# Attention arithmetic on pairs of token tiles, with the projection, the transposes and the index conversions re-ordered around it

## The reference

```
mod = silu(c) @ wmod -> sa, ca, ga, sb, cb, gb        (ga, gb kept at least 0.25 away from zero)
h = layernorm(x) * (1 + ca) + sa
a = groupnorm( tanh( relu( rope(h @ W_Q) ) + hh_b ) )  (32 groups of 16 channels; rope on the first 64 channels)
x = x + ga * transpose(a)                              (tokens and channels swapped, read back as B,T,C)
h = layernorm(x) * (1 + cb) + sb
x = x + gb * ( (silu(h @ Wg.T) * (h @ Wu.T)) @ Wd.T )  (Wg, Wu, Wd: 1376 x 512, each entry lut[idx], 16 table values)
```

## Time and profile before

| | |
|---|---|
| median of 3 runs | 1054.35 us (1053.17 to 1059.23) |
| profiled execution | 1054.04 us, its span 1051.8 us |
| PE busy | 943.4 us, 90% of the span |
| DVE busy | 602.9 us, 57% |
| ACT busy | 414.1 us, 39% |
| POOL busy | 185.0 us, 18% |

### The profile page before, as it was taken

One profiled execution on the slowest core, in us unless ns is written; L12 is line 12 of the kernel. 1 busy time (PEld: TensorE's weight loads), 2 busy tenths in 40 slices (PEclk: granted clock), 3 DMA queues, 4 the chain that ended last, 5 costly groups with the idle time before them and its releaser, 6 DMA issues.

```text
span 1051.8 us, 12874 instructions
## 1 busy us (share of the span) xinstructions
PE 943.4 (90%) x4364; PEld 435.4 (41%) x4364; DVE 602.9 (57%) x1375; ACT 414.1 (39%) x627; POOL 185.0 (18%) x156
## 2 busy tenths in 40 slices
PE   5777569877898979999898899999999999999998
PEld 1233334333343434444444444444444444444443
DVE  5896999975888953335878876322222432222312
ACT  3482857483665633224552532222222421222200
POOL 3130202053565632012211200110000100000000
PEclk8889698998999999999999999999999999999999
DMA  8659356410000031124235214222000112000011
GB/s 272 180 139 309 75 177 202 117 55 26 21 30 20 20 120 61 44 97 121 58 102 160 40 41 160 81 79 82 0 0 1 61 41 100 0 0 0 1 41 41
DMA packets 33738, 83.44 MB, mean 79 GB/s; under 512 B 2848, under 2 KB 2976, under 8 KB 30624
## 3 DMA queue, kind: packets, MB, share of 16 engines
q1 hardware_dynamic: 32544, 74.54, 21.4%
q0 software_dynamic: 1152, 8.39, 4.3%
HBM read 64.04 MB, written 18.87 MB: 79 GB/s over the span
## 4 chain that ended last, share of the span: by engine, by line
PE 65%; DVE 18%; issue 6%; ACT 6%; POOL 2%; DMA 2%; SPq 1%; DVEq 0%; ACTq 0%; POOLq 0%
PE ps L1191 28%; PE ps L1225 22%; PE ps L1158 6%; DVE hid L854 3%; PE ps L1180 3%; DVE R L876 2%; PE ps L1203 2%; PE ps L1146 2%; DVE st L770 1%; DMA xa<-x_dram 1%; DVE hd L885 1%; ACT R L578 1%; ACT h L517 1%; DVE xa L865 1%; POOL work L434 1%
## 5 line engine op out<-in xcount | busy, mean ns | idle before, releaser
L1191 PE MATMUL ps<-h,w_all 128*128 128x512 f16 x1920 | 424.8, 383 | 18.8 <-DVE hd L885 16.3
L1191 PEld LDWEIGHTS ps<-h,w_all 128*128 (+1 forms) x1920 | 188.6, 99 | 252.3 <-issue 19.9
L1225 PE MATMUL ps<-w_all,hid 128*128 128x512 f16 x1056 | 231.1, 381 | 4.7 <-DVE w_all L1075 4.7
L1225 PEld LDWEIGHTS ps<-w_all,hid 128*128 128x128 f16 x1056 | 103.5, 98 | 129.6 <-DVE w_all L1075 5.2
L885 DVE SCALAR_TENSOR_TENSOR hd<-ps,col,sg 128x512 f32<-128x512 f32 x80 | 59.8, 748 | 154.7 <-ACT sg L539 154.7
L539 ACT ACTIVATE sg<-ps,col 128x512 f32<-128x512 f32 x80 | 54.6, 682 | 181.8 <-PE ps L1191 181.2
L910 DVE SCALAR_TENSOR_TENSOR hd<-ps,col,gbB 128x512 f32<-128x512 f32 x32 | 24.0, 751 | 148.4 <-PE ps L1225 148.1
L1180 PE MATMUL ps<-hid,w_all 128*128 128x512 f16 x352 | 90.8, 422 | 12.1 <-DVE hid L854 11.1
L554 ACT ACTIVATE hid<-hd 128x512 f16<-128x512 f32 (+1 forms) x88 | 55.0, 628 | 112.9 <-DVE hd L885 99.6
L1158 PE MATMUL ps<-WQ,work 128*128 128x512 f16 x384 | 89.7, 396 | 7.0 <-POOL work L434 7.0
L434 POOL TENSOR_TENSOR h<-h,h 128x512 f16<-128x512 f32 x32 | 37.4, 1188 | 306.2 <-ACT h L524 306.2
(11 more groups left out here) (115 smaller groups left out, 786.3 us busy)
## 6 DMA issues: line engine op xcount, KB each, us to landing
R<-x_dram SPq DMA_DIRECT2D x16, 1024.0 KB, 6.9
xa<-x_dram SPq DMA_DIRECT2D x14, 1024.0 KB, 6.1
hid<-idx_dram SPq DMA_DIRECT2D x44, 256.0 KB, 5.6
R<-bias_dram POOLq DMA_DIRECT2D x8, 1024.0 KB, 8.3
out_dram<-R SPq DMA_DIRECT2D x32, 256.0 KB, 2.2
x_dram<-R SPq DMA_DIRECT2D x7, 1024.0 KB, 5.1
w_all<-wmod_dram SPq DMA_DIRECT2D x6, 1024.0 KB, 13.2
h<-idx_dram SPq DMA_DIRECT2D x11, 256.0 KB, 2.6
```

What stands on the lines that cost most here:

```text
L1191: ins = nc.tensor.matmul(bank(GU[2 * s + t]), W[wp][:, bass.ds(at, P)], h2[hp][:, s, k], start=(k == 0 and i == 0), stop=(k == K - 1 and i ...
L1225: ins = nc.tensor.matmul(bank(QY[par]), hid[hp][:, bass.ds(at, P)], W[wp][:, w_at:w_at + BLK], start=(j == 0 and i == 0), stop=(j == J - 1 ...
```

## The change

It joins instructions in pairs of tiles and re-orders the four engines' `attn_block`s:

- `rope_relu`, `center`, `sum_squares` (VectorE) and `tanh`, `square` (ScalarE) take two tiles each. A pair waits for both tiles of the step before it. Rope is now four products of 128x64 with strides instead of two of 128x2x32 for each tile.
- `project` is called in halves of 24 matmuls, with a `sum_chunk` (first stage, from block 1 on) or a `gate_up` (group 1) between them.
- `stats` of the next block moves ahead of the first `center` (from block 1 on); the squares come later on ScalarE, behind `norm` and `summed_out`.
- in the first stage, `transpose_x` and `affine` of the next block come in halves with a chunk's work between.
- the indices of chunks 19, 20 and 21 are converted by ScalarE instead of POOL, which keeps 17 and 18.
- of the three modulation loads of 1 MB that SP issued in block 0, SB goes out in block 1, CB and GB in block 2.

```diff
-        ACT_IDX = AHEAD * NB + 1
+        POOL_IDX = (AHEAD * NB + 1, AHEAD * NB + 2)
...
-                if q == 0:
-                    for s in (SB, CB, GB):
-                        load_mod(s)
+                for s in ((), (SB,), (CB, GB), ())[q]:
+                    load_mod(s)
...
+            def tanh(n, pair):
+                a = 2 * pair
+                act.wait_ge(pre_tanh, A * n + a + 2)
+                nc.scalar.activation(H[:, a:a + 2], H[:, a:a + 2], ACT.Tanh, scale=c_isq).then_inc(tanh_ready, 2)
...
+                reach(act, sq_summed, A * n + a)
+                nc.scalar.activation(sq[:], H[:, a:a + 2], ACT.Square).then_inc(squared, 2)
...
+            def rope_relu(n, q, pair):
+
+                a, half = 2 * pair, ROPE // 2
                 reach(dve, pre_tanh, A * n + a)
-                dve.wait_ge(q_ready, A * n + a + 1)
...
+                reach(dve, sq_summed, A * n)
+                dve.wait_ge(q_ready, A * n + a + 2)
...
+                for e in range(2):
+                    Qe = Q[:, :, 0:ROPE].rearrange("p a (i e) -> p e a i", e=2)[:, e]
+                    v.tensor_tensor(rot[:, e], Qe, table(cosT), ALU.mult)
+                    ins = v.tensor_tensor(tmp[:, e], Qe, table(sinT), ALU.mult)
...
-            def project(n, m, y_before):
-
-                pe.wait_ge(lo_ready, K * (m + 1))
-                reach(pe, o_ready, y_before)
-                for a in range(A):
-                    reach(pe, q_taken, A * n + max(a - 1, 0))
+            def project(n, m, y_before, pair):
+
+                if pair == 0:
+                    pe.wait_ge(lo_ready, K * (m + 1))
+                    reach(pe, o_ready, y_before)
+                reach(pe, q_taken, A * n + 2 * pair)
+                for a in (2 * pair, 2 * pair + 1):
...
             half_idx(w + 2, 0)
             split_lo(LN_B[0], h2[0][:, 0], h2[1][:, 0])
-            half_idx(w + 3, 1)
-            half_idx(w + 4, 0)
-            split_lo(LN_B[1], h2[0][:, 1], h2[1][:, 1], (0,))
-            half_idx(w + 5, 1)
-            split_lo(LN_B[1], h2[0][:, 1], h2[1][:, 1], (1,))
+            split_lo(LN_B[1], h2[0][:, 1], h2[1][:, 1])
```

More of the change, by code:

```diff
@@ L613, in attn_block @@
                 half_idx(w + 3, 1)
-                tanh(q, 1); square(q, 0); tanh(q, 2); square(q, 1)
+                if q:
+                    if not last:
+                        norm(q + 1)
+                    summed_out(w, 0)
+                square(q, 0)
+                tanh(q, 1)
                 if q == 0:
-                    tanh(q, 3)
                     act.wait_ge(row_ready, 1)
                     make_bias(0)
+                    norm(q + 1)
+                    summed_out(w, 0)
+                summed_out(w + 1, 1)
+                square(q, 1)
                 if not last:
-                    norm(q + 1)
-                if q:
-                    tanh(q, 3)
-                summed_out(w, 0)
-                square(q, 2); square(q, 3)
-                if not last:
+                    affine(q + 1, CA, SA, 0, hq[0], lambda: act.wait_ge(q_ready, A * q + A), halves=(0,))
                     half_idx(w + 4, 0)
-                summed_out(w + 1, 1)
-                if not last:
-                    affine(q + 1, CA, SA, 0, hq[0], lambda: act.wait_ge(q_ready, A * q + A))
+                    summed_out(w + 2, 0)
                     half_idx(w + 5, 1)
+                    affine(q + 1, CA, SA, 0, hq[0], lambda: None, halves=(1,))
                 else:
@@ L633, in attn_block @@
                     copy_mod(2, (SB, CB, GB))
-                summed_out(w + 2, 0)
+                    summed_out(w + 2, 0)
                 if not last:
@@ new lines, in rope_relu, with center @@
+                over = lambda t: t.unsqueeze(1).broadcast_to((P, 2, t.shape[1]))
+                v.scalar_tensor_tensor(H[:, a:a + 2, ROPE:], Q[:, :, ROPE:], 0.0, over(hhS[:, ROPE:]),
+                                       ALU.max, ALU.add).then_inc(q_taken, 2)
+                v.scalar_tensor_tensor(H[:, a:a + 2, 0:ROPE], gs[:, 2].rearrange("p (a n) -> p a n", a=2), 0.0,
+                                       over(hhS[:, 0:ROPE]), ALU.max, ALU.add).then_inc(pre_tanh, 2)
+            def center(n, pair):
+                a = 2 * pair
+                dve.wait_ge(tanh_ready, A * n + a + 2)
+                Hg = H[:, a:a + 2].rearrange("p a (g e) -> p (a g) e", e=GSZ)
+                sums = gs[:, 0, a * GRP:(a + 2) * GRP]
@@ L1018, in attn_block @@
                 masks(w + 1, 1)
-                rope_relu(q, q, 0); rope_relu(q, q, 1); center(q, 0); rope_relu(q, q, 2); center(q, 1)
+                rope_relu(q, q, 0)
+                if q and not last:
+                    stats(q + 1)
+                center(q, 0)
+                rope_relu(q, q, 1)
+                sum_squares(q, 0)
                 if q == 0:
-                    rope_relu(q, q, 3)
                     gates_of_attn()
-                if not last:
                     stats(q + 1)
-                if q:
-                    rope_relu(q, q, 3)
-                sum_squares(q, 0); center(q, 2); sum_squares(q, 1); center(q, 3)
+                center(q, 1)
                 if not last:
                     masks(w + 2, 0)
-                sum_squares(q, 2); sum_squares(q, 3)
+                sum_squares(q, 1)
                 if last:
@@ L1278, in attn_block @@
                 sum_chunk(w, 0, True)
+                if not gates:
+                    project(q, q, 0, 1)
                 sum_chunk(w + 1, 1)
@@ L1284, in attn_block @@
                 else:
-                    transpose_x(q + 1, q)
+                    transpose_x(q + 1, q, halves=(0,))
                 sum_chunk(w + 2, 0)
+                if not last:
+                    transpose_x(q + 1, q, halves=(1,))
                 if last:
```

94 lines of the change are left out of this document (42 added, 52 removed).

## The result

The changed kernel takes 1075.04 us (median of four runs, 1067.28 to 1079.58) against 1055.41 us (four runs of the kernel before). The ratio is 1.0176, 95% interval 1.0142 to 1.021: slower by 1.8%. The forecast was 1057 us with a range of 1046 to 1064. So the sign of the small change was right, its size was far off, and the measured time lies above the range. The profiled execution took 1073.19 us with a span of 1071.4 us, 19.6 us longer than before.

The account below looks back on a forecast made before the run. VectorE's chain was taken to bound the attention blocks and the transition. The terms +4.1 - 5.5 + 2.85 + 3.8 - 5.0 + 3.0 = +3.3 us on 1054.04 gave 1057 us, range 1046 to 1064.

Parts of the forecast that it names:

- The transition, -5.0: Between batch 0's blocks and the feed-forward part: ScalarE's conversions end the masks' wait for POOL, saving 5.0 us.
- the sum of chunk 19 starts 2.3 us sooner, from 238.0 to 241.5: Transition: with masks no longer waiting for POOL, PE sets the pace and runs this sum in 3.5 us without pauses.
- third rival: Transition: no gain, since ScalarE's in-order queue holds conversions behind norm and affines behind conversions; 1062 us, chance 0.15.
- Block 0, +4.1: Batch 0, first block: rope waits for 24 matmuls, second square stands behind norm and two copies; 4.1 us longer.
- Block 2, +2.85: Batch 0: 5.4 us of new VectorE idle time against 1.6 saved, less 0.51 for a conversion; 2.85 us longer.
- block 1, -5.5: Batch 0: without three modulation loads in front of xa, the block gets block 2's period, 44.1 instead of 49.6 us.
- lands 8.2 us later, t = 9.5: Block 2's head: xa arrives 8.2 us after its issue, so VectorE idles 1.9 us before the statistics.
- the halves cost nothing: Batch 0: affine's second half comes about 5 us ahead of its reader, half transposes fill PE's idle time; zero cost.
- Block 3, +3.8: Batch 0, last block: no statistics fill waits for tanh, the projection's second half and the second square; 3.8 us longer.
- Batch 1, +3.0: Four blocks: +1.0 us in two, +0.6 in the first, +0.4 in the last; 3.0 us longer in all.
- the saved VectorE time arrives: Rival: the blocks' waits are filled and each of eight blocks gains 1.6 us; fully 1028 us, half 1047; chance 0.18.
- xa lands late: Rival: moved loads meet xa, statistics start 4.7 us later in block 2 or also block 1; 1062 to 1067, chance 0.17.

Follow-up runs that it names:

- e2: Kernel before, with only the transition's edit: chunks 19, 20 and 21 converted by ScalarE instead of POOL; 1053.74 us, ratio 0.9979.
- e11: Kernel before with modulation loads later, the transition's conversions on ScalarE, and transposes and affine in halves in batch 0; 1049.82 us, ratio 0.9933.
- e13: The best kernel (before, with modulation loads spread and the transition's conversions on ScalarE) with the change's blocks in batch 1 alone; 1052.28 us, ratio 0.9953.
- e3: Changed kernel, order and halves kept, with rope, center, square, tanh and sum of squares on one tile per instruction again; 1064.66 us, ratio 1.0078.
- e8: Kernel before with modulation loads later (SB in block 1, CB and GB in block 2) and the transition's conversions on ScalarE; 1048.39 us, ratio 0.9927.
- e15: The best kernel (before, with modulation loads spread and the transition's conversions on ScalarE) with the change's blocks in blocks 1 and 2 of batch 0; 1054.66 us, ratio 0.9978.
- e6: Changed kernel with squares (and the second tanh in blocks 1 to 3) ahead of the copies of sums on ScalarE in batch 0; 1075.74 us, ratio 1.019.
- e1: Kernel before with only the modulation loads later: SB in block 1, CB and GB in block 2; 1053.67 us, ratio 0.9966.
- e12: Kernel before with the transition's conversions on ScalarE and modulation loads spread (SB, GB behind residual rows, CB behind chunk loads); 1046.72 us, ratio 0.9906.

## Why the prediction was wrong

**What failed is the sum, by terms that were all too small on the same side.** The structure was right: waits in the heads of the blocks, each as long as the saving, and the saving itself as priced. Between the forecast +3.3 us and the measured 19.6 the transition was short by 2.9 us, batch 1 with what follows it by 2.8, block 0 by 2.7, block 2 by 2.4, group 0 by 2.2, block 3 by 1.7 and block 1 by 1.6. Term by term:

- *The transition, -5.0.* It gave -2.1, alone (e2) as with the rest. The step that failed is "the sum of chunk 19 starts 2.3 us sooner, from 238.0 to 241.5". In e2, less the 1.1 us by which block 3 began later, that sum ran from 239.1 to 244.4. It began late because PE's queue had the last transposes in front of it and these waited for ScalarE's affine; ScalarE worked without a gap from the conversion of 19 (226.9 in e2, at the end of the masks of 17, which read the same buffer) up to that affine. And it took 5.3 us instead of 3.5, at a granted clock of 0.68. The walk named PE as next but not what PE's own queue waits for. The masks at 4.70 us beside POOL, which the walk gave 2.8, were not what held it: those of 19 were done 4.9 us before the sum, and those of 21 waited 4.4 us for PE. So the third rival's mechanism, ScalarE's conversions in front of its affines, was there; its size, no gain at all, was not.
- *Block 0, +4.1.* It cost +6.8. The step that failed, as far as the walk's few words show, is the one that took the 48 matmuls as one stretch: a joined rope frees both banks together, so the second half started at 46.37, 2.30 us after the first was done, and rope 1 waited 1.50 us. `group_scale` starts some 2 us later than put.
- *Block 2, +2.85, and block 1, -5.5.* They gave +5.2 and -3.95. The step that failed is "lands 8.2 us later, t = 9.5". xa took 9.9 and 9.1 us, so the statistics started at t = 11.1 and 10.6, and everything behind them was late by as much; this is 1.6 of block 2's 2.4 us and 1.1 of block 1's 1.6. "The first pair needs 24 matmuls, half of the 10.53 us" failed as well in block 2 (6.88 us, rope at t = 7.0), but nothing hung on it there: the rope was done before xa came. I had slower first matmuls in batch 1's walk, where the window's clock was 0.96, and did not ask about them in block 2, whose own was 0.88. At the tail of both, the eight masks at 4.68 us next to POOL's subtraction ate the conversion's 0.5 us that I had subtracted; this was "the halves cost nothing", wrong for the row and not told apart from nothing in the time (e11).
- *Block 3, +3.8.* It cost +5.5, taking the transition's -2.1 from e2. Here nothing is loaded and PE is what the head waits for: the first 24 matmuls took 5.83 us, 2.29 us stood in front of rope 0 and 2.40 in front of rope 1.
- *Batch 1, +3.0.* +4.2 in its blocks, of which 2.7 in the last, put at +0.4. That block has no statistics to cover the second half of the projection, and rope 1 waits 3.5 us. Another +1.6 stands behind it, "the rest" of the table, put at nothing: PE waits 2.5 us for the last residual, and the 12 matmuls behind that wait take 4.28 us at a granted clock of 0.64 instead of 2.75 at 1.00. e13, with batch 1 changed alone, has both again (+4.4 and +1.3 by its stages, 5 us by its time).
- *Feed-forward group 0, put at nothing.* +2.25 us. It holds the same work and varies by more than that between profiles; see the last section.

**The rivals.** That the saved VectorE time arrives was given 0.18. Its saving is real (11.8 us of busy time) and never reached the end: e3 shows that with the joining undone the kernel is 10 us faster, not 13 slower. The Trainium skill (Perfetto Trace Analysis, Optimizing Scalar/DVE Operations) says that grouping can improve throughput if the engine is saturated. Here e3 does not agree, although VectorE was busy for 39.0 of block 2's 41.3 us; our reading is that it was full of a chain and not of independent work. *xa lands late* came in part. In the changed kernel it moved the statistics of blocks 1 and 2 by 1.1 and 1.6 us, where the rival had 4.7, and it sets their pace; in e8 xa took 12.1 us. In e15, with no modulation load near, xa of block 2 took 12.3 us as well and VectorE waited 5.37 us: POOL's transfer of bias rows went out at 127.76, 1.2 us ahead of xa's, as in e6's block 1, and 4.6 us ahead of it in block 2 of the changed kernel.

**Settled and open.** Settled: the loads and the transition are worth 0.9927; the new order with the halves, nothing joined, costs some 1.5% on top (1.0078), and joining another 1.0%. The loss lies in every stage where the new blocks run, by the times about 5 us in block 0, in block 3 and in batch 1, 8 in blocks 1 and 2. Argued from rows, not shown by a run of its own: how block 0's loss divides between the banks and the second square, that an earlier xa would shorten blocks 1 and 2, and that ScalarE's queue is what holds the transition. Open: how the costs of joining rope and of joining the rest overlap.

## What to carry to other kernels

Joining two tiles in one instruction saves its overhead and delays the first tile to the readiness of the second; in a chain over several engines that delay is paid at each hand-over (matmul, rope, tanh, center, square), and two tiles in two banks leave the producer no free bank. Join where both inputs lie ready and something independent stands behind; here 12 us of VectorE's time saved (e3 against the changed kernel) came with a kernel 10 us slower, so the added waits cost some 22. Moving a reader ahead of the work that covered its load puts the load on the chain: blocks 1 and 2 then followed xa's landing. Before a stage is put at the length that it has in a trace, ask what its engine did before it and what runs beside it: both the 24 matmuls after a wait and the masks beside POOL were longer than the same work elsewhere, by 29% and by 69%. And split a bundle: the two edits outside of the blocks, which the bundle hid, made the kernel 0.7 to 0.9% faster.

## What the runs showed of the hardware

The same feed-forward group 0, with the same instructions, took from 226.1 to 232.1 us in the 18 profiles. Windows over it for the kernel before, e1 and e15:

```profile
256.16:483.89 227.73, 205.38 (x936) 91.93 (x937) 136.93 (x274) 103.27 (x155) 87.73 (x66) 0.96 0.16 55
```
```profile
251.30:483.42 232.12, 208.65 (x936) 92.93 (x937) 136.88 (x274) 103.12 (x155) 87.63 (x66) 0.94 0.16 54
```
```profile
260.19:486.27 226.08, 203.55 (x936) 91.64 (x937) 137.14 (x274) 103.24 (x155) 87.70 (x66) 0.97 0.16 55
```

VectorE, ScalarE and POOL are busy for the same time; PE's busy time and its granted clock (0.94 to 0.97) differ. So 2 to 4 us of an upstream gain can vanish or appear. In e1 the feed-forward part starts 4.9 us sooner, and its group 0 is 4.4 us longer. What decides the share of full clock isn't shown, and the start alone does not: e12 and e13 begin group 0 at 246.2 and 246.3 us and take 231.7 and 230.0 us for it. Stage periods of one profile are therefore safer than its total, and a gain of less than 0.5% needs many runs. What comes behind batch 1's last block is the opposite case: 413.66 to 413.74 us in eleven profiles, and 414.9 to 415.4 in the seven where the first 12 matmuls of it take 4.0 to 4.4 us instead of 2.75.

Eight masks of 1024 elements take 2.77 us alone and 4.68 to 4.70 us beside POOL's subtraction. In e3 one set kept its 2.77 us although a subtraction stood ready (171.35, with masks from 169.69): there POOL's two instructions stretched to 3.23 us instead.

```profile
169.69 2.77 DVE L877 TENSOR_SCALAR hid<-hid 128x1024 f16<-128x1024 f16 x8
171.35 3.23 POOL L439 TENSOR_TENSOR work<-h,work 128x512 f16<-128x512 f32 x2 [8.95 <-ACT work L525]
```

So one or the other pays. What decides isn't shown: in block 2 of the changed kernel the masks were also ahead, by 1.5 us (173.21 against 174.70), and took 4.68. The period of that block was 44.1 us in e3 against 46.5; how much of it is this isn't shown either.

A load of 1 MB, xa, landed 8.2 us after its issue in block 2 of the kernel before, 11.7 and 12.1 us with a modulation load 5.2 and 6.2 us ahead of it (block 2 of e1 and e8), and 12.3 us with POOL's transfer of bias rows 1.2 and 1.7 us ahead (block 2 of e15, block 1 of e6).
